# The last stage of a four-stage model kernel: an order of operations computed across passes, and six shared work banks

## The reference, cut to what matters

```python
gh = relu(einsum('bsd,hd->bsh', x, gfc1_w) + gfc1_b)
g = (einsum('bsh,eh->bse', gh, gfc2_w) + gfc2_b).mean(axis=1)
W1m = W1 + einsum('be,efd->bfd', g, tv_W1)
b1m = b1 + g @ tv_b1
W2m = W2 + einsum('be,edf->bdf', g, tv_W2)
b2m = b2 + g @ tv_b2
h = relu(einsum('bsd,bfd->bsf', x, W1m) + b1m[:, None, :])
out = einsum('bsf,bdf->bsd', h, W2m) + b2m[:, None, :]
res = x + out
...
return (res - mu) * rsqrt(var + LN_EPS) * lng + lnb
```

## Time and profile before

| what | value |
|---|---|
| median of 3 runs | 2277.54 us (lowest 2277.15) |
| the profiled execution's own time | 2281.0 us |
| its span, first to last instruction | 2278.1 us |
| last stage within the span | from 1684.5 to 2278.1 us |
| PE busy over the span | 2023.2 us, 89% |
| DVE busy over the span | 1577.6 us, 69% |
| mean granted TensorE clock | 0.962 |

### The profile page before, as it was taken

The page is one execution under the profiler, slowest core; times in us unless marked ns, Lnnn a source line. Parts: engine busy times, 40 slices in busy tenths (PEclk is TensorE's granted clock), DMA queues, the critical chain, the costliest instruction groups (busy, mean ns, idle before and its releaser), DMA issues. The chain is left out here.

```text
span 2278.1 us, 57687 instructions
## 1 busy us (share of the span) xinstructions
PE 2023.2 (89%) x19468; PEld 1493.1 (66%) x19468; DVE 1577.6 (69%) x4533; ACT 1256.7 (55%) x2588; POOL 1058.1 (46%) x1135
## 2 busy tenths in 40 slices
PE   5989898889868999999994899999978888988897
PEld 2655555555546777777772666666647777777776
DVE  4999999999962222223223799999957777787776
ACT  4766666666632222222223788888845554555553
POOL 4577777777666100000006777877601233222333
PEclk9999999999978999999996999999979999999999
DMA  3122222222115555555552311111100000000000
GB/s 90 49 68 67 67 68 69 65 63 65 54 37 172 159 163 167 162 156 157 164 161 61 124 41 39 38 39 39 33 6 6 15 21 16 15 15 16 20 19 20
DMA packets 97009, 159.76 MB, mean 70 GB/s; under 512 B 19074, under 2 KB 49931, under 8 KB 96756
## 3 DMA queue, kind: packets, MB, share of 16 engines
q1 hardware_dynamic: 66036, 79.53, 12.3%
q0 software_dynamic: 30848, 78.56, 11.4%
HBM read 113.06 MB, written 44.96 MB: 69 GB/s over the span
## 5 line engine op out<-in xcount | busy, mean ns | idle before, releaser
L1292 DVE TENSOR_SCALAR b_hT<-b_hbank,b_w 128x512 f32<-128x512 f32 (+1 forms) x156 | 105.7, 678 | 368.7 <-PE b_hbank L1236 368.6
L344 POOL DMA_INDIRECT sent<-a_xn_mid,a_pos_cur x256 | 253.1, 989 | 81.8 <-issue 81.6
L1466 POOL DMA_INDIRECT c_rows<-done,c_cur_pos x256 | 245.5, 959 | 75.6 <-issue 74.8
L1266 ACT ACTIVATE b_hT<-b_hbank,b_w 128x512 f32<-128x512 f32 (+1 forms) x156 | 98.3, 630 | 322.7 <-PE b_hbank L1236 322.7
L1246 PE MATMUL b_bank<-b_w,b_hT 128*128 128x128 f32 x2160 | 254.2, 275 | 2.1 <-DVE b_hT L1292 2.1
L1246 PEld LDWEIGHTS b_bank<-b_w,b_hT 128*128 128x128 f32 x2160 | 247.5, 192 | 2.4 <-DVE b_hT L1292 2.3
L1236 PE MATMUL b_hbank<-b_xT,b_w 128*128 128x512 f32 (+1 forms) x624 | 246.9, 539 | 1.1 <-DMA b_w<-pack_dram 1.1
L1212 POOL DMA_DIRECT2D done<-b_y x78 | 42.5, 545 | 423.1 <-DVE b_y L1300 405.0
L2219 PE MATMUL d_bank<-d_g_diag,tv 64*128 64x112 f32 x2368 | 167.1, 291 | 34.2 <-DVE d_wm L2419 29.5
L2219 PEld LDWEIGHTS d_bank<-d_g_diag,tv 64*128 64x128 f32 x2368 | 155.0, 199 | 46.6 <-ACT d_wm L2322 34.5
L2419 DVE COPY d_wm<-d_bank 128x448 f32<-128x448 f32 (+1 forms) x152 | 148.5, 1024 | 50.4 <-PE d_bank L2219 48.2
(11 more groups left out here) (256 smaller groups left out, 4516.5 us busy)
## 6 DMA issues: line engine op xcount, KB each, us to landing
b_w<-pack_dram SPq DMA_DIRECT2D x78, 258.0 KB, 2.7
b_w<-pack_dram SPq DMA_DIRECT2D x78, 256.0 KB, 2.7
b_x<-sent SPq DMA_DIRECT2D x57, 256.0 KB, 2.7
done<-b_y POOLq DMA_DIRECT2D x57, 256.0 KB, 2.4
out_dram<-h_all SPq DMA_DIRECT2D x32, 256.0 KB, 2.3
b_b<-pack_dram SPq DMA_DIRECT2D x78, 64.0 KB, 1.9
tv<-tv_dram SPq DMA_DIRECT2D x1, 4736.0 KB, 15.6
sent<-a_xn_mid,a_pos_cur POOLq DMA_INDIRECT x256
```

The source lines that it names most:

```text
L344: pool.indirect_dma_start(out=sent_d, out_offset=bass.IndirectOffsetOnAxis(ap=pos_cur[:, g.par, b, k:k + 1], axis=0), in_=xn_mid[:, g.par, ...
L1466: pool.indirect_dma_start(out=rows[:, g.par, b, k, :], out_offset=None, in_=done_d, in_offset=bass.IndirectOffsetOnAxis(ap=cur_pos[:, g.pa ...
```

## The change

Only merged_phase changes, and with it the layout in which the stacked weights arrive.

1. **Layout.** Each half of the partitions now holds half of W1's blocks followed by half of W2's (SHARE = 37 blocks of each). Both engines copy first their share of W1 (fills 0 to 9) and then their share of W2 (fills 10 to 19). There are 20 fills a pass instead of 19; fills 9 and 19 hold one block.
2. **Banks.** Banks 0 to 5 are one pool, named work, that serves merge, up, turn_x, gate_hidden, the gate and the bias; banks 6 and 7 are the output banks. The bank of each use is written beside it.
3. **Order.** The operations of every engine stand in an order that crosses the turn of a pass. step(p) takes work of the passes p - 1, p and p + 1. On TensorE the first 11 fills of pass p + 1 stand between and behind the last downs of pass p, and the step ends there.
4. **Steps.** run_passes now issues steps -1, 0, 1 written out, steps 2 to 5 as a loop of two trips over two steps, and steps 6 to 9 written out.
5. **Waits.** Inside the loop a use of a bank waits for the one operation that emptied it last. In the written-out steps it waits for every user of that bank (cleared), each at its latest turn. The lists users0 to users5 hold 13, 15, 15, 12, 13 and 14 entries, together 82, which is also the number of bank uses in a pass.

```diff
-        h_bank, out_bank, turn_bank, gate_bank = (ps[0:2], ps[2:4]), ps[4:6], ps[6], ps[7]
+        work, out_bank = ps[0:6], ps[6:8]
...
         def run_passes(eng, step):
...
+            for n in range(-1, 2):
+                step(Pass(n, n % 2, n // 2))
+            with eng.Fori(0, (PASSES - 4) // 2) as j:
+                step(Pass(j * 2 + 2, 0, j + 1))
+                step(Pass(j * 2 + 3, 1, j + 1))
+            for n in range(PASSES - 2, PASSES + 2):
+                step(Pass(n, n % 2, n // 2))
...
+            users3 = ((kept[1], 20, -1, 12), (kept[1], 20, -1, 15), (kept[0], 20, -1, 18), (relued[1], 16, -1, 1), (relued[1], 16, -1, 5), (xT_ready, 4, 0, 1), (relued[0], 16, -1, 8), (relued[1], 16, -1, 12), (relued[1], 16, -1, 15), (kept[1], 20, 0, 3), (kept[1], 20, 0, 6), (kept[1], 20, 0, 9))
...
+            def cleared(p, users, place):
+
+
+                for i, (read, each, off, k) in enumerate(users):
+                    n = min(p.n + off - (i >= place), PASSES - 1)
+                    if n >= 0:
+                        pe.wait_ge(read, n * each + (k + 1))
...
+            def step(p):
+                if q := p.at(-1):
+                    if p.is_edge():
+                        cleared(p, users2, 0)
+                        cleared(p, users5, 0)
+                    else:
+                        pe.wait_ge(kept[0], q.n * 20 + 9)
+                        pe.wait_ge(kept[1], q.n * 20 + 9)
+                    merge(q, 11, (work[2], work[5]))
...
+                    up(q, 15, (work[0], work[3]))
+                    down(q, 13)
+                if q := p.at(0):
...
+                    merge(q, 0, (work[5], work[2]))
...
+                    merge(q, 1, (work[1], work[4]))
+                if q := p.at(-1):
+                    down(q, 14)
...
+            def keep(q, k, bank):
+
+                act.wait_ge(filled[0], q.n * FILLS + (k + 1))
+                if k == 0 and q.is_past(1):
+                    act.wait_ge(up_full[1], q.n * SEQS)
+                if k == HALF_FILLS and q.is_past(1):
+                    act.wait_ge(down_done, q.n * SEQS)
...
+    up, down = by_block(up), by_block(down.reshape(E + 1, FF, P))
+    return np.concatenate([np.concatenate([w[:, h * SHARE:(h + 1) * SHARE] for w in (up, down)], axis=1) for h in range(2)])
```

## The result

The changed kernel takes 2312.1 us (median of 4 runs, 2309.2 to 2312.7) against 2279.4 us for the kernel before (median of 4 runs, one of them at 3790.5 us, the other three from 2277.2 to 2281.3). The ratio without that one is 1.0144, 95% interval 1.0124 to 1.0164. The forecast was 2263 us with a range of 2218 to 2305: the sign was wrong, and the time lies 7 us above the range. Each kernel has one profiled execution, and that of e3 alone fell among the slower executions of its kernel, so its figures are used only beside those of e1 and e4.

A forecast was written before the change was run, and what follows sets the result against it. No engine was full; the sum of their turns set the length, PE bounding up and down. Last-stage terms summed to 578.7 us against 593.6, saving 14.9: 2266 from the profiled execution, 2263 us as median, range 2218 to 2305.

The forecast's parts named there:

- the sign: Whole kernel: the change was forecast to be faster, last stage 578.7 us against 593.6, a saving of 14.9.
- the loop pass of 62.5 us: Steps 2 to 5: copies 19.6, up and down 41.5, less 1.8 for two downs, plus 0.7 and 2.5 for stalls.
- the computed order stalls: Rival, chance 0.15: late normalisations delay relus in VectorE's queue; 67 us a pass, about 30 us more, 2293 us.
- The waits: TensorE's written-out steps: each wait takes 0.11 us of the sequencer; steps 6 and 7 come to 78.3 us each.
- 32.4 less 19.6: Merge of a written-out step: 271 waits plus passing products take 32.4 us, against 19.6 for the copies.
- bursts that nothing covers: Rival, chance 0.10: wait bursts in up and down outlast PE's queued work; 114 us more, 2377 us; half, 2320.
- Hidden waits: Rival, chance 0.17: waits cost only 51 ns and hide behind copies, all passes like the loop's; 61 us less, 2216 us.
- 19.6 + 0.7: Merge in the loop: back-to-back copies take 19.6 us, plus 0.7 for last copy and first relu before the first down.
- 2.5 us were set aside for stalls: Loop pass: an estimated 2.5 us for stalls of the present kind, since every engine's order changes.
- The branches: Loop of the last stage: one branch back and one out instead of three, 2 us added to the four loop passes.
- The clock rival: Rival, chance 0.03: PE's clock falls to 1.2 GHz, four up and down parts cost about 41 us each; 2390 us and more.

The follow-up runs named there:

- e3: Changed kernel with one swap in VectorE's normalisation order, all waits kept; last stage 591.1 us, 22.8 less than the changed kernel.
- e1: Changed kernel with TensorE's redundant waits left out, only the largest new value per semaphore kept; last stage 556.5 us, ratio to the kernel before 0.986.
- e4: Changed kernel with both few TensorE waits and the one swap in VectorE's order; last stage 534.2 us, 79.7 less than the changed kernel.
- e7: Few-waits version of the changed kernel, with GpSimd's three closing instructions on one of four sequences; 2204.7 us, last stage 507.4.
- e12: The changed kernel with few waits, nothing else, the same kernel as e1 run on another chip; 2251.6 us, ratio 0.9885, last stage 558.1.
- e8: Kernel before with 12 satisfied waits added ahead of each of the 19 fills of all eight passes; 2319.1 us, ratio 1.0182.
- e10: e9 with group 3's last normalisation moved behind the next pass's group 1 normalisation, group 0 restoring and residual; 2204.2 us, ratio 0.967, last stage 505.3.
- e11: e9 with the change's own loop of two trips instead of written-out passes; 2213.1 us, ratio 0.972, last stage 517.7.
- e9: e4 with the loop written out and group 2's last normalisation moved behind the restoring of group 3; 2204.9 us, ratio 0.968, last stage 511.7.

## Why the prediction was wrong, point by point

The runs split the 44.3 us that the forecast missed. In the measure of the experiments the forecast is 569.6 us (578.7 less the 9.1 ahead of the first transposes), and 523.2 with waits that cost nothing.

| part | forecast, us | measured, us | from |
|---|---|---|---|
| stage without wait cost and without contention | 523.2 | 512.1 | e7, with 4.7 for the full closing |
| DVE beside GpSimd's instructions | 0 | 46.0 | e12 less the line above |
| waits | 46.4 | 55.8 | changed less e12 |
| sum | 569.6 | 613.9 | |

- **The failed step is the loop pass of 62.5 us**, in its clause that DVE's 55.1 us fit below it and GpSimd's 19.6 by far. I compared each engine's total with the pass, as if they could run side by side. They can't: where a normalisation met an instruction of GpSimd it took two to four times as long. DVE's work grew to 59.5 us a pass in the loop, and, what cost more, it grew ahead of the transposes, the relus and the first copies that PE waits for. So the engines of this kernel wait for one another not only through semaphores, as the description of the chip says: here VectorE is held behind GpSimd with no semaphore between them. The sign of the outcome hangs on it: without the 46 us the changed kernel would have come out faster than before. By the Trainium skill, page "SBUF — State Buffer", section "SBUF: two separate sides", VectorE and GpSimd share a port pair as an exclusive lock, held for the whole instruction, when VectorE's instruction is in a mode that uses two ports or has two inputs in SBUF. The traces agree in that a stretched normalisation ends with GpSimd's instruction, and e7 agrees: with the closing cut to a quarter the stretch fell from 66 us above the bare 71 to 18. That the normalisations run in such a mode no trace shows. Not all of VectorE's work is held: in the changed kernel its relus take 344 ns where GpSimd's instructions overlap them and 345 elsewhere, the statistics of a row (BATCH_NORM_STATS2) 279 and 276, and a full copy out of a bank takes 1080 ns (1057 before).
- **It could have been read before.** The trace of before has 507 ns for a normalisation into xn and 340 for one into res, the same instruction on the same shape. That gap was the contention, 18 us in all: 28 of the 256 normalisations met an instruction of GpSimd there, and those took 1.01 us on average. A computed order that moves these instructions should have been laid against GpSimd's closings.
- **The rival "the computed order stalls" (0.15) came nearest**: 67 us a pass, 2293 us, with late normalisations as its reason. Without the waits the seven steps of e12 take 66.9 us on average. It named what PE would wait for, but not why it would be late: it held DVE behind the closings in the order, and nothing in it makes an instruction longer. Its price of 30 us was too low, and since the waits were already in the 2263 it was added on top of them as it should be.
- **The waits were right in their price.** 0.11 us each was forecast; e8 gives 0.114. The two merges that are written out wholly took 34.9 and 35.8 us, against 21.9 and 22.9 in e12: 13 us for the waits, where the forecast had 32.4 less 19.6. The whole term came out at 55.8 instead of 46.4 us. The up and down parts of steps 6 and 7, forecast at 3 us each, grew by 3.9 and 5.7, and with the stalls came more half clock: steps 6 and 7 have a granted clock of 0.95 and 0.90. How much of the 9.4 us is the clock no run separates.
- **The rival "bursts that nothing covers" was rightly small.** The ups of the last steps stand 0.2 us for "issue", not over 1 us, save where another stall had emptied PE's queue. "Hidden waits" is excluded by e8.
- **The banks and the order were better than forecast.** Merges of 20.5 to 20.8 us (19.6 + 0.7 forecast) and passes of 59.2 to 61.5 in e10, where almost nothing meets, instead of 62.5; 2.5 us were set aside for stalls that an order need not have. That the merges fit is in part luck: the copy of 1.02 to 1.05 us came from rows that mix full and half fills, and a full copy on DVE takes 1.06 us before and 1.13 in e10.
- **The branches** were put at 2 us for the loop. The pass with the branch back is some 10 us longer (e11: 70.9 against 60.3). I took PE's 1.69 us and did not ask where the other engines branch.
- **The clock rival** as such did not come. Its price was also added up too low: four parts at 41 us more each are 164 us on 2263, about 2425, not 2390. But half-clock stretches behind stalls of 1 to 3.5 us were part of most terms: PE's granted clock over the stage is 0.93, 0.95 before, 0.97 in e10. Only the loop's last step, at 1.00, had none.

How the 46.0 us of contention split can be read from the two rows of e12 and e7: TensorE is busy 10.4 us less in e7 for the same products (492.66 and 482.26), most likely what the half clock behind its stalls cost, and it stands 35.6 us less. The 46.0 us are a lower bound, since e7 keeps 18 us of stretched instructions; e10, with the closings whole and its loop written out, takes 505.3 us. What stays open: that the two-port mode is the reason, as said above, and e10's order with the loop kept, which was not tried.

## What to carry to other kernels

Lay the engines' orders beside each other, not only each against its total: a run of VectorE's normalisations, or of like instructions from SBUF to SBUF, must not stand where GpSimd works on SBUF, and the sign of it is one instruction with two mean durations in the same profile. Wait once for the largest value of each semaphore; a satisfied wait costs 0.11 us of TensorE's sequencer and is free only while the burst is clearly shorter than the work queued. When engines leave a loop at different places in their orders, each branch back is a stall of its own.

## What the runs showed of the hardware that I had not expected

- A satisfied wait on TensorE's queue costs 0.114 us of issue (e8), twice the 51 ns that its row shows, and it costs more than its own time where a half-clock stretch follows the stall.
- One 128x128 normalisation takes 0.34 us alone and up to 1.43 us beside a GpSimd tensor operation (changed kernel), and the stretched one ends 81 to 88 ns behind GpSimd's end, in all 72 cases. GpSimd's operation itself is not slower: 1.27 us on average for 128x512, in the changed kernel and in e10.
- The branch back of a loop held VectorE for 2.47 us and TensorE for 2.72 us. The Trainium skill, page "Advanced Engine Details and Errata", section "Control Flow Timing", gives some 108 ns for compare-and-branch; VectorE's branch row is that short (74 ns), but its next instruction starts 2.8 us later, and TensorE's row is 3.4 us long. The measurement decides.
- Written-out passes instead of the loop cost nothing that shows: the last stage is 6.0 us shorter (e9 against e11, one execution each).
